# Butterfly coefficients laid side by side by GpSimd before TensorE reads them, with the late down stages, the second square and the down side's turning moved

## What is computed

```
r_t = 0.9 * r_(t-1) + ctx_t * ctx_t            (along each sequence)
x   = x + layernorm(x) * r_t
h   = layernorm(x) @ W_exp + b_exp             (512 -> 2048)
h   = butterfly(h, up_weights)                 (11 stages of 2x2 blocks)
h   = gelu(h + up_bias)
h   = butterfly(h, down_weights)               (11 stages)
x   = x + h @ W_con + b_con + down_bias        (2048 -> 512)
```

## Time and profile before

| what | value |
|---|---|
| runs shown | 2771.31, 2770.5, 2771.94 us |
| profiled execution | 2771.06 us |
| its span, first to last instruction | 2769.2 us |
| PE busy | 2740.1 us (99%) |
| DVE, ACT, POOL busy | 2122.9 (77%), 1131.0 (41%), 396.5 us (14%) |
| granted clock of PE, mean over the span | 0.995 |

### The profile page before, as it was taken

How to read it: one execution, slowest core, us unless ns; L and a number is a source line. 1 busy time by engine, 2 the same in 40 slices (tenths; PEclk the granted TensorE clock), 3 DMA queues, 4 the chain that set the end, 5 groups by cost and what they waited for, 6 DMA issues and landing times.

```text
span 2769.2 us, 35072 instructions
## 1 busy us (share of the span) xinstructions
PE 2740.1 (99%) x12191; PEld 2260.4 (82%) x12191; DVE 2122.9 (77%) x3554; ACT 1131.0 (41%) x1715; POOL 396.5 (14%) x561
## 2 busy tenths in 40 slices
PE   8899999999999999999999999999999999999998
PEld 6778888888888888888888888888888888888887
DVE  9878787778878777787877878787787877778533
ACT  5743434334343433434343343434434343343432
POOL 4712011110201111010110101011020111102000
PEclk8999999999999999999999999999999999999999
DMA  9795765758576575856757585675857557584543
GB/s 275 266 294 152 216 191 167 228 154 240 165 204 203 168 213 155 255 163 195 201 170 223 155 239 168 190 214 162 235 152 224 185 175 223 161 243 152 182 149 99
DMA packets 292021, 540.48 MB, mean 195 GB/s; under 512 B 36918, under 2 KB 98518, under 8 KB 274950
## 3 DMA queue, kind: packets, MB, share of 16 engines
q1 hardware_dynamic: 285456, 535.77, 64.7%
q10 hardware_dynamic: 5414, 1.25, 0.3%
q0 software_dynamic: 976, 1.22, 0.2%
HBM read 445.83 MB, written 60.82 MB: 183 GB/s over the span
## 4 chain that ended last, share of the span: by engine, by line
PE 98%; ACT 1%; issue 0%; DVE 0%; DMA 0%; ACTq 0%
PE ps L1767 44%; PE ps L1788 25%; PE ps L1801 25%; PE ps L1664 1%; PE ps L1570 1%; PE ps L1642 0%; PE ps L1668 0%; ACT wcon L863 0%; PE ps L1662 0%; ACT w1r L885 0%; PE ps L1670 0%; PE ps L1868 0%; DMA wexp<-in_L_ffn_W_exp_dram 0%; PE ps L1716 0%; PE ps L1589 0%
## 5 line engine op out<-in xcount | busy, mean ns | idle before, releaser
L1767 PE MATMUL ps<-xop,w1r 128*128 128x512 f32 x5376 | 1364.1, 389 | 2.5 <-DVE xop L1296 1.6
L1767 PEld LDWEIGHTS ps<-xop,w1r 128*128 128x128 f32 x5376 | 1008.8, 188 | 212.7 <-DVE xop L1296 2.0
L1788 PE MATMUL ps<-w2r,ghi 128*128 128x512 f32 x2048 | 630.5, 389 | 0.0
L1801 PE MATMUL ps<-w2r,ghi 128*128 128x512 f32 x2032 | 625.8, 389 | 0.0
L1002 ACT ACTIVATE st<-ps 128x512 f32<-128x512 f32 x384 | 229.7, 598 | 839.9 <-PE ps L1767 839.9
L1403 DVE TENSOR_TENSOR x<-ps,x 128x512 f32<-128x512 f32 x508 | 348.6, 686 | 280.6 <-PE ps L1801 278.2
L1788 PEld LDWEIGHTS ps<-w2r,ghi 128*128 128x128 f32 x2048 | 384.4, 188 | 79.8
L1801 PEld LDWEIGHTS ps<-w2r,ghi 128*128 128x128 f32 x2032 | 381.2, 188 | 79.8 <-DVE glo L1426 0.4
L1421 DVE TENSOR_TENSOR g<-ps,st 128x512 f32<-128x512 f32 x384 | 262.9, 685 | 212.5 <-PE ps L1767 212.1
L1006 ACT ACTIVATE g<-g,gelu_bias 128x512 f32<-128x512 f32 x384 | 275.4, 717 | 362.7 <-DVE g L1421 361.6
L1426 DVE TENSOR_TENSOR glo<-g,ghi 128x512 fp32r<-128x512 f32 x510 | 347.5, 702 | 79.9 <-ACT ghi L1020 79.8
(11 more groups left out here) (174 smaller groups left out, 1701.8 us busy)
## 6 DMA issues: line engine op xcount, KB each, us to landing
w1r<-w_products SPq DMA_DIRECT2D x889, 256.0 KB, 3.3
w2r<-w_split SPq DMA_DIRECT2D x126, 1024.0 KB, 5.0
x<-in_x_dram SPq DMA_DIRECT2D x128, 256.0 KB, 7.2
raw<-kv SPq DMA_DIRECT2D x480, 64.0 KB, 2.2
out_dram<-x SPq DMA_DIRECT2D x120, 256.0 KB, 4.0
kv<-in_ctx_dram SPq DMA_DIRECT2D x64, 256.0 KB, 7.3
raw<-in_ctx_dram SPq DMA_DIRECT2D x64, 256.0 KB, 5.3
wexp<-in_L_ffn_W_exp_dram SPq DMA_DIRECT2D x4, 1024.0 KB, 10.9
```

The source lines that it names most:

```text
L1767: last = nc.tensor.matmul(bank[:, :], w1r[:, slot, w, c * P:(c + 1) * P], xop[:, XPOS[m], v, c, :], start=(opens and i == 0), stop=(i == l ...
L1788: last = nc.tensor.matmul(ps_ya[j][:, :], g[:, p % 2, q, j * P:(j + 1) * P], w2r[:, p % 2, kk, w, :], start=(p == 0 and kk == 0 and i == 0 ...
L1801: last = nc.tensor.matmul(ps_yb[:, :], g[:, p % 2, q, j * P:(j + 1) * P], w2r[:, p % 2, kk, w, :], start=(kk == 0 and i == 0), stop=(kk == ...
```

## The change

It has five parts.

1. POOL copies the coefficients of low stages 2 and 3 and of the four high stages so that the halves `bit` = 0 and 1 lie side by side (`lay_dense`, `dense_lows`, `dense_highs`): two copies per stage, 24 in all. `stage_spread` reads these copies. PE waits for them by new semaphores.
2. PE spreads the down side's stages 4 and 5 with the other low ones, ahead of the down side's high spreads, and no longer after step 3 of `high_up`; the down side's `top` spreads stand behind step 8 of `high_up` instead of step 9. With this, SP's condition for loading `wcon` counts 16 spreads instead of 20.
3. ACT's second square moves from behind step 6 of `high_up` to behind step 15, the last.
4. DVE does `high_products(0)` ahead of `stats1(0, 0)`.
5. `turn_low` becomes a PE transpose with the plain identity; the permutation is done by ACT as it empties the bank.

```diff
+        dense_high = [flat(HX[:, 0, 0:8, :]), flat(WT[:, 0:2, :])]
+        dense_low = [(Z[:, 15, 2 * P:4 * P], Z[:, 9, :]), (WT[:, 2, 0:2 * P], WT[:, 3, :])]
...
-        SPREAD_ORDER = (list(range(LOWS + HIGH)), [*range(PARTED[0]), *range(LOWS, LOWS + HIGH), *PARTED])
...
             if kind == "turn_low":
-                return LX[:, 1, 4 * i:4 * i + 4, :].rearrange("p a b -> p (a b)"), whole
+                return LX[:, 1, 4 * i:4 * i + 4, :].rearrange("p a (r e) -> p a r e", e=E),\
+                    whole.rearrange("p (a e r) -> p a r e", a=4, e=E)
...
+            def lay_dense(dst, src, order, ready):
+                half_n = dst.shape[1] // 2
+                v = src.rearrange(order, o=KH, a=2, b=2)
+                for bit in range(2):
+                    to = dst[:, bit * half_n:(bit + 1) * half_n]
+                    nc.gpsimd.tensor_copy(to.rearrange("q (o a l) -> q o a l", o=v.shape[1], a=2), v[:, :, :, :, bit])\
+                        .then_inc(ready, 1)
...
             load_coefs(pool, down_w, 1)
             nc.gpsimd.memset(parts_zero(1), 0.0).then_inc(parts_zeroed[1], 1)
+            dense_lows(0)
             load_high(pool, down_w, 1)
...
+            pool.wait_ge(sel_rounded, 2)
+            pool.wait_ge(top_sel_ready, 4)
+            dense_highs(0)
+            pool.wait_ge(fold_made, fold_at("low_up", 3) + 1)
+            dense_lows(1)
+            dense_highs(1)
             pool.wait_ge(fold_made, fold_at("low_up", KH - 1) + 1)
             nc.gpsimd.memset(top_parts[1].bitcast(f32), 0.0).then_inc(top_zeroed, 1)
...
             for r in range(R):
                 fold_step("high_up", r)
+                if r == R - 1:
+                    square(0, 1)
                 if r == 6:
-                    square(0, 1)
...
+            high_products(0)
             stats1(0, 0, xs[0], range(J))
-            high_products(0)
...
-                        last = nc.tensor.matmul(o, LX[:, 1, 4 * i + c, :], rank_major(ident[:, :]), start=True, stop=True)
+                        last = nc.tensor.transpose(o, LX[:, 1, 4 * i + c, :], ident[:, :])
...
-            spread_low_dn(range(PARTED[0]))
+            spread_low_dn(range(LOWS))
             spread_high_dn(range(HIGH))
...
                 fold_step("high_up", r)
-                if r == 3:
-                    spread_low_dn(PARTED)
-                if r == 9:
+                if r == 8:
                     spread_top_dn((0, 1, 2, 3))
```

More of the change, by code:

```diff
@@ L219, in xattn_ffn_program @@
         sel_rounded = sem("sel_rounded")
+        dense_low_ready = [sem("dense_low_up_ready"), sem("dense_low_dn_ready")]
+        dense_high_ready = [sem("dense_high_up_ready"), sem("dense_high_dn_ready")]
         parts_zeroed = [sem("parts_up_zeroed"), sem("parts_dn_zeroed")]
@@ L368, in spreads @@
             return dn * (LOWS + HIGH) + stage + 1
-        SPREAD_ORDER = (list(range(LOWS + HIGH)), [*range(PARTED[0]), *range(LOWS, LOWS + HIGH), *PARTED])
         def spread_count(dn, stage):
-            return dn * (LOWS + HIGH) + SPREAD_ORDER[dn].index(stage) + 1
+            return dn * (LOWS + HIGH) + stage + 1
         UP_DONE = LOWS + HIGH
@@ L697, in choose, with dense_lows, dense_highs @@
                         .then_inc(sel_ready, 1)
+            def lay_dense(dst, src, order, ready):
[5 more added lines that the diff above has]
+                        .then_inc(ready, 1)
+            def dense_lows(dn):
+                pool.wait_ge(low_loaded[dn], LOW_LOADS * NX)
+                for stage in PLAIN:
+                    rows, off, n = src_place(stage)
+                    lay_dense(dense_low[dn][stage - PLAIN[0]][0:rows], low_src[dn][0:rows, off:off + n],
+                              "q (o l a b) -> q o a l b", dense_low_ready[dn])
+            def dense_highs(dn):
+                pool.wait_ge(high_loaded[dn], HIGH_LOADS * NX)
+                for b in range(HIGH):
+                    rows, off, n = src_place(b)
+                    lay_dense(dense_high[dn][0:rows, off:off + n], high_src[dn][0:rows, off:off + n],
+                              "q (l o a b) -> q o a l b", dense_high_ready[dn])
             def choose_high(b):
@@ L1564, in spread, with stage_spread @@
             def spread(dn):
-                def stage_spread(src, place, stage, choice, order):
-                    rows, off, n = src_place(stage)
+                def stage_spread(dense, place, n, rows, choice):
                     bank, col = place
-                    v = src[0:rows, off:off + n].rearrange(order, o=KH, a=2, b=2)
                     for bit in range(2):
                         last = nc.tensor.matmul(ps[bank][:, col:col + n // 2], sel[0:rows, choice, bit, :],
-                                                v[:, :, :, :, bit], start=(bit == 0), stop=(bit == 1))
+                                                dense[:, bit * (n // 2):(bit + 1) * (n // 2)],
+                                                start=(bit == 0), stop=(bit == 1))
                     last.then_inc(coef_spread, 1)
@@ L1622, in low @@
                             pe.wait_ge(sel_ready, 2 * (LOWS - stage))
-                            stage_spread(low_src[dn], LOW_PLACE[stage], stage, HIGH + stage - PLAIN[0], "q (o l a b) -> q o a l b")
+                            rows, _, n = src_place(stage)
+                            pe.wait_ge(dense_low_ready[dn], 2 * (stage - PLAIN[0] + 1))
+                            stage_spread(dense_low[dn][stage - PLAIN[0]][0:rows], LOW_PLACE[stage], n, rows,
+                                         HIGH + stage - PLAIN[0])
                 def high(stages):
-                    pe.wait_ge(high_loaded[dn], HIGH_LOADS * NX)
+                    pe.wait_ge(dense_high_ready[dn], 2 * HIGH)
                     pe.wait_ge(sel_ready, 2 * (len(PARTED) + len(PLAIN) + HIGH))
@@ L1630, in high @@
                     for b in stages:
-                        stage_spread(high_src[dn], HIGH_PLACE[b], b, b, "q (l o a b) -> q o a l b")
+                        rows, off, n = src_place(b)
+                        stage_spread(dense_high[dn][0:rows, off:off + n], HIGH_PLACE[b], n, rows, b)
                 return low, high, top
```

## The result

| | median us | lowest to highest | runs |
|---|---|---|---|
| before | 2771.38 | 2770.5 to 2773.13 | 20 |
| changed | 2775.68 | 2774.5 to 2777.96 | 20 |

A forecast was written before the change was run, and what follows sets the result against it. DVE, with the smaller slack, was taken to bound the prologue. Copies +2.6, square +1.1, clock +1.8 and `turn_low` -2.5 gave +3.0 on the profiled 2771.06, 2774.1, or 2774.3 us as median; range 2769.3 to 2779.

The forecast's parts named there:

- Copies, +2.6 on DVE: Prologue: POOL's 24 new copies delay DVE's work beside them by 2.6 us; bounds 0 and +9.7.
- The square, net +1.1: Second scan: DVE waits 3.9 us for ACT's late square; after 2.81 spare, +3.7 remain, 2.6 being the copies.
- Clock, +1.8: Top spreads: PE idles 3 to 7 us before them, then runs at half clock, +1.8 us; bounds 0 and +3.6.
- Part 1 and 2 on PE, 0: PE's spreads before the top spreads: denser reading and earlier stages end in PE waiting for DVE, 0 us directly.
- `turn_low`, -2.47: Before `tokens_lo(0, 0)`: PE gains 5.2 us, but DVE waited only 2.47 for ACT, so -2.47 us; other bound 0.
- Part 4, 0: DVE's products ahead of statistics: DVE's sum stays, only ACT's 0.27 us is in it, so 0.
- Every copy paid: Rival, prologue: DVE waits for each POOL copy's whole length, +9.7 in place of +2.6, 2781 us; chance 0.24.
- the chain at its word: Rival, prologue: PE sets the pace, so 5.2 us of `turn_low` and at least 3 of spreads go, 2763; chance 0.05.
- Cheap copies: Rival, prologue: copies slip between DVE's locks, PE waits 1 us and keeps its clock, 2769.9 to 2772; chance 0.27.

The follow-up runs named there:

- only DVE is late: The change with the square behind step 8 and DVE's first transpose of `raw` waiting until ACT has evicted all of `turn_high`: 2775.08 us.
- only ACT late: The change with the square behind step 8 and four unused copies (2.1 us) on ACT behind step 15 of `high_up`: 2775.16 us.
- the added products: The change plus 16 more products of 128 columns on PE ahead of the top spreads, to keep it busy: 2778.52 us.

## Why the prediction was right, and where it was wrong

The forecast was 2774.3 us and slower by a little; it is 2775.68. The sum came out 1.3 us short (+3.0 against +4.3) through errors that partly cancel, so part of the nearness is luck: 2.47 us were credited to `turn_low`, which brought 0.2 by itself, and copies, square and clock were put at 5.5 us, where some 4.5 were paid if `turn_low` brought as little here.

- **Copies, +2.6 on DVE.** Right in size as far as it shows: DVE's top products start 2.81 us late (68.75 against 65.94). Of this 1.35 lie between the first transpose of `kv` and there (33.3 us before, 34.7 after), where I had 1.1. That is firm: the six kernels with the old order and no copies have 33.32 to 33.35 us there, six with copies 34.6 to 34.9. (The two with the new order and no copies have 34.9 as well, since DVE waits there for PE's strided spreads.) The other 1.46 lie ahead, where I had 1.5, and there a late load can't be told from the copies. POOL's copies took 12.7 us where I had 11.2. Not all of that is the copies' own: the same copies take less in other traces. By form, busy us and mean ns of one, in after and (last row) with the square early:

```profile
L708 POOL COPY WT<-wcon 16x128 f32<-16x128 f32 x2 | 1.7, 873 | 0.0
L708 POOL COPY WT<-HX 64x32 f32<-64x32 f32 x2 | 1.4, 712 | 0.0
...
L708 POOL COPY WT<-HX 64x32 f32<-64x32 f32 x2 | 0.4, 200 | 0.0
```

  Beside them DVE's scan took 1.57 and 1.54 us against 1.22, and `lane_rows(0)` 1.59 against 0.68. The Trainium skill (SBUF — State Buffer, Who interferes with whom) has the loser wait for the whole instruction; charged to every copy, that was my rival of 2781 us. The slower steps agree with such a wait; but DVE paid 2.8 of 12.7 us at most, so most of the copies' time held nothing up. In the median the copies are worth 0 to 1.1 us.
- **The square, net +1.1.** This is the step that failed. DVE's wait was as forecast (5.90 us; I had 3.9, and 5.7 with the clock), but "before it reaches 89.06 it had 2.81 us to spare" treated ACT's group at 88.40 as fixed. I had noted that `turn_high` and four evictions stand behind the square, and put no price on it. The 2.81 us vanish where only DVE is late; with ACT late too 1.49 of them stay, and with only ACT late 2.70. The square alone costs 3.9 us, not 1.1, and each of its two routes alone 2.7, although each absorbs 2 us or more. I had also given all of the slack to the square; the copies alone use up more than half of it (1.18 us are left) and cost little.
- **Clock, +1.8.** The mechanism is there, PE idle for 4.06 us and then at 0.50, but the top spreads took 3.33 us, not 3.9. Full clock there, less the 0.8 us for which the added products held the spreads up, moved the square by some 0.7 us and didn't lower the median. This term isn't confirmed. What the sum had no term for is the bias product, ahead of ACT's first high halves: 6.46 us in after and 3.99 with the square early, at granted clocks of 0.53 and 0.89. That is 2.5 of the 5.9 us by which these halves are late.
- **Part 1 and 2 on PE, 0.** Right: 1.3 us shorter for a high set at full clock (I had said 2), all of it waited away.
- **`turn_low`, -2.47.** Wrong alone (-0.2): DVE's wait for ACT was real, but ACT ran into its stores, and with those moved into POOL's sums. The wait ahead of `tokens_lo` fell to 0.83 us as forecast, and that showed no gain, since DVE itself was late. Only with ACT's work moved forward did it bring 1.1.
- **Part 4, 0.** Not tested by itself; the kernel that has it beside `turn_low` and the earlier spreads, with the square early and without copies, is at 2772.10, so nothing large is in it.
- **The rivals.** Every copy paid (2781) fell, and so did the chain at its word (2763). Cheap copies was nearer to the truth on the copies than the forecast, but it had taken the square for cheap as well.

## What to carry to other kernels

A wait of 2.8 us in one engine's row is slack only if the engine that ends it stays where it is: before counting it, ask whether the change also moves that one. A long instruction moved on an engine is late for its reader and for all that is queued behind it; price both, here evictions, a matmul step, a product and high halves. And where two engines pass buffers back and forth through stores, look for the engine that does the most work in the stretch (ACT here, 35 of 42 us) and for an idle stretch just ahead of it that its later work could fill.

## What the runs showed of the hardware

- At full clock a strided fp32 moving operand, four numbers apart, costs PE a half more: 16 records in 3.90 us, and 2.58 with dense halves, each in five or more traces with a granted clock of 1.00 throughout. (In the kernel before the clock falls to 0.50 at the end of the 3.90 us, from about 45.9 on, and the time is the same.) At half clock the stride costs next to nothing. The down side's high set, strided in the kernel before and dense with the square early, both at 0.50:

```profile
51.85 4.84 PE L1570 MATMUL ps<-HX,sel 64*128 64x32 f32 x16
...
53.73 4.76 PE L1601 MATMUL ps<-WT,sel 64*128 64x32 f32 x16
```

- The clock fell to 0.50 behind 4.06 us of idle PE. It also falls where PE never rests, during the one-column bias product, which starts at 77.82 us in the kernel before (columns as above):

```profile
77.00:79.00 2.00, 2.00 (x21) 1.93 (x19) 1.97 (x2) 1.74 (x4) 1.92 (x2) 1.00 0.00 0
79.00:81.00 2.00, 2.00 (x15) 2.00 (x16) 1.90 (x5) 0.00 (x0) 1.92 (x4) 0.75 0.00 0
81.00:83.00 2.00, 2.00 (x10) 2.00 (x11) 1.97 (x3) 0.32 (x1) 1.92 (x3) 0.50 0.00 0
```

  The time of the product follows the mean clock over it: 3.63 us at 1.00 (no copies, square early), 4.83 at 0.73 (before), 6.46 at 0.53 (after), 6.82 at 0.50 (only ACT late).
- POOL's copies of 2048 numbers have a least time that grows with the columns: 200 ns for 64x32, 252 for 32x64, some 400 for 16x128 and some 620 for 8x256. Above it the same copy varies from trace to trace: 200 and 712 ns for the 64x32 into `WT`, 406 and 874 for the 16x128 from `wcon`. Neither its form nor its place is the reason, then; what ran beside it is the likely one, which wasn't tried.
- The stores of 1024 KB to `w_products` took 4.8 to 5.2 us from issue to landing (medians of four each, before and after), so a pair of staging places handed on by high halves, low halves and store is held longest by the store.
